# The squares of layer 0's embeddings, summed by ScalarE instead of VectorE, in a two-layer graph network kernel

## The reference

```
layer 0:
  t1    = x @ W1
  msg   = (t1[src] + (x[src] * x[dst]) @ W2) / (sqrt(deg[src]) * sqrt(deg[dst]))
  embed = where(in_cnt > 0, t1 + segment_sum(msg, dst), 0) + b
  embed = leaky_relu(embed, 0.01)
  embed = embed / max(norm(embed, axis=1), 1e-12)
  x1    = layernorm(x + embed)
layer 1:
  out   = segment_sum((x1 @ W.T + b)[src], dst) / (deg + 1)
  y     = layernorm(x1 + out)
```

## Time and profile before

| | |
|---|---|
| Runs | 3945.45, 3954.75, 3956.32 us |
| Median | 3954.75 us |
| Span of the profiled execution | 3955.7 us |
| Busy share TensorE (matmul) | 76% |
| Busy share VectorE | 47% |
| Busy share ScalarE | 17% |
| Busy share GpSimd | 75% |
| Mean granted TensorE clock | 0.742 of full speed |
| Gathers of L585, layer 0 | 1270, from 372.2 us on |
| Gathers of L585, layer 1 | 1540, from 2004.5 us on |

### The profile page before, as it was taken

The page is one execution under the profiler, slowest core; times in us unless marked ns, Lnnn a source line. Parts: engine busy times, 40 slices in busy tenths (PEclk is TensorE's granted clock), DMA queues, the critical chain, the costliest instruction groups (busy, mean ns, idle before and its releaser), DMA issues.

```text
span 3955.7 us, 56274 instructions
## 1 busy us (share of the span) xinstructions
PE 3009.0 (76%) x10186; PEld 1878.7 (47%) x10186; DVE 1854.3 (47%) x3529; ACT 671.9 (17%) x2118; POOL 2958.4 (75%) x3112
## 2 busy tenths in 40 slices
PE   4551887888877778788877888878788878877787
PEld 4441565655556656566534344434444434433443
DVE  9994455555555555555432323233333233323333
ACT  8991111111111111111100000000000000000000
POOL 7776777777777777777757777777777777777776
PEclk5555788888888888887857666677767777677767
DMA  7878455555555555555434444444444444444443
GB/s 254 269 236 318 134 159 158 155 159 160 156 158 158 160 156 160 157 165 157 135 89 118 121 123 122 122 122 122 121 121 121 123 122 121 121 122 122 122 121 107
DMA packets 306368, 588.12 MB, mean 149 GB/s; under 512 B 65107, under 2 KB 189178, under 8 KB 306170
## 3 DMA queue, kind: packets, MB, share of 16 engines
q0 software_dynamic: 148416, 405.47, 35.1%
q1 hardware_dynamic: 144986, 168.09, 12.7%
q10 hardware_dynamic: 12768, 12.85, 0.9%
HBM read 506.24 MB, written 75.45 MB: 147 GB/s over the span
## 4 chain that ended last, share of the span: by engine, by line
POOL 66%; issue 23%; POOLq 1%; DMA 1%; DVE 0%; DVEq 0%; PE 0%; ACT 0%; SPq 0%; ACTq 0%
POOL ring L585 66%; POOLq L582 0%; DMA ring<-scaled_x,idx 0%; DVEq L808 0%; DMA ring<-x,idx 0%; POOLq L583 0%; PE banks L1264 0%; POOL ring L595 0%; DMA x<-out_t 0%; DVE stats L1039 0%; POOLq L627 0%; DMA result<-out_t 0%; DVE out_t L1051 0%; ACT scal L738 0%; POOLq L96 0%
## 5 line engine op out<-in xcount | busy, mean ns | idle before, releaser
L1264 PE MATMUL banks<-ring,hot_space 128*128 128x257 f32 x6252 | 2399.0, 512 | 728.3 <-DMA ring<-x,idx 363.4
L1264 PEld LDWEIGHTS banks<-ring,hot_space 128*128 128x128 f32 x6252 | 1298.5, 238 | 1744.6 <-DMA ring<-x,idx 966.8
L585 POOL DMA_INDIRECT ring<-x,idx x1540 | 1462.1, 949 | 493.7 <-issue 469.2
L585 POOL DMA_INDIRECT ring<-scaled_x,idx x1270 | 1221.2, 962 | 396.5 <-issue 393.7
L970 DVE SCALAR_TENSOR_TENSOR big<-banks,here_mask,big 128x257 f32 x784 | 343.3, 479 | 1693.6 <-PE banks L1264 1693.6
L926 DVE TENSOR_TENSOR hot_space<-banks,dst_rel 128x1024 f32<-128x1024 f32 x392 | 479.6, 1225 | 181.8 <-issue 180.0
L708 ACT COPY idx<-src_col 128x8 int32 (+1 forms) x392 | 77.2, 197 | 2238.8 <-PE banks L1264 2238.8
L595 POOL DMA_INDIRECT ring<-in_x,src_col x276 | 264.9, 960 | 84.1 <-issue 84.1
L671 ACT ACTIVATE dst_rel<-columns,halves 128x128 bf16<-128x128 f32 x960 | 268.3, 375 | 4.6 <-DVE halves L843 4.6
L1163 PE MATMUL banks<-hot_space 128*128 128x98 bf16 x1088 | 101.2, 282 | 132.2 <-DVE hot_space L815 132.2
L1229 PE MATMUL banks<-w_s,a_t 128*128 128x256 f32 x784 | 195.7, 406 | 0.0
(11 more groups left out here) (121 smaller groups left out, 1169.6 us busy)
## 6 DMA issues: line engine op xcount, KB each, us to landing
src_lo<-x SPq DMA_DIRECT2D x2944, 1.0 KB
kept_rows<-ring SPq DMA_DIRECT2D x94, 384.0 KB, 3.2
ring<-kept_rows SPq DMA_DIRECT2D x47, 768.0 KB, 6.0
ring<-x,idx POOLq DMA_INDIRECT x1540, 2.8
src_lo<-scaled_x SPq DMA_DIRECT2D x1408, 1.0 KB
ring<-scaled_x,idx POOLq DMA_INDIRECT x1270, 2.8
dst_col<-in_src SPq DMA_DIRECT2D x47, 384.0 KB, 6.7
scaled_x<-big ACTq DMA_DIRECT2D x14, 896.0 KB, 17.3
```

The lines of the kernel that those rows point to most:

```text
L585: g.indirect_dma_start(ring[:, u, 0:D], None, table[layer], bass.IndirectOffsetOnAxis(ap=idx[:, u:u + 1], axis=0)).then_inc(rows_in[u], 16)
L1264: last = nc.tensor.matmul(group_sum(k % SUMS), dst_hot[:, k % HOTS, u - k * GT, :], ring[:, u, 0:DW], start=u == tiles[0], stop=u == tiles ...
```

## The change

VectorE no longer squares. It increments a semaphore once the leaky relu is done. In `roots` ScalarE waits for that semaphore, increments its own `act_turn`, runs two activations with the function Square over the pair's embeddings, each with its row sums going to the column of `scal` that the root reads, drains, and takes the root as before. The output of the Squares goes to `out_t`, as that of L1003 did. Nothing else changes.

```diff
             def roots(layer, m):
                 if layer == 0:
-                    act.wait_ge(square_ready, m + 1)
+                    act.wait_ge(embed_ready, m + 1)
+                    act.sem_inc(act_turn, 1)
+                    for s in range(2):
+                        nc.scalar.activation(out_t[s][:, :], e[s][:, :], ACT.Square, accum_out=scal[:, 2 + s:3 + s])
+                    act.drain()
                     nc.scalar.activation(pair[2], pair[1], ACT.Sqrt).then_inc(norm_ready, 1)
...
                         nc.vector.scalar_tensor_tensor(e[s][:, :], e[s][:, :], 0.01, e[s][:, :], ALU.mult, ALU.max)
                     ordered()
-                    for s in range(2):
-                        nc.vector.tensor_tensor_reduce(out=out_t[s][:, :], in0=e[s][:, :], in1=e[s][:, :], scale=1.0,
-                                                       scalar=0.0, op0=ALU.mult, op1=ALU.add,
-                                                       accum_out=scal[:, 2 + s:3 + s])
-                    ordered()
-                    v.sem_inc(square_ready, 1)
+                    v.sem_inc(embed_ready, 1)
```

More of the change, by code:

```diff
@@ L267, in gnn @@
         projected = sem("projected")
-        square_ready = sem("square_ready")
+        embed_ready = sem("embed_ready")
         norm_ready = sem("norm_ready")
```

## The result

The kernel after takes 3964.68 us (median of 11 runs, 3963.89 to 3966.67); the kernel before, beside it on the same chip, 3956.01 (11 runs, 3945.45 to 3957.1). The ratio is 1.0024 [1.0015, 1.0032]: slower by 8.7 us, which is less than the 0.3% bound of the prediction and over the top of its range, 3963. The profiled executions have spans of 3964.6 and 3955.7, 8.9 apart, so the two traces hold the difference.

A forecast was written before the change was run, and what follows sets the result against it. The prediction took GpSimd's gathers and the pause ending layer 0 as the bound. Stalls 0 plus end of layer 0 +0.7 gave 3956.4 on the 3955.7 span, carried to the median as 3955.5 us; range 3945 to 3963.

The forecast's parts named there:

- 0.3% bound of the prediction: Whole kernel: 11.9 us, about what a measurement can tell from no change; slower by more was given 0.05.
- I take 0 for all stalls together, -4.8 to +4.2 as bounds: Layer 0's gathers: stalls removed and stalls gained by the shift cancel, net 0 us, between -4.8 and +4.2.
- a replay of layer 0 alone: Layer 0's stall rule replayed with VectorE lines shifted -0.2 to +0.8: 11.8 to 20.8 us of stalls, 16.6 unshifted.
- -1.76 for L1003: Layer 0's gather path: removing the VectorE squares takes away their 16 gather stalls, -1.76 us.
- L1035 and L982 might give it back: Layer 0: these VectorE lines slide onto gather starts, as likely as not giving back L1003's 1.8 us.
- the standing beat: Rival, slower: L1035 and L982 stall gathers nearly every round, up to 0.32 us each, 3969 us; chance 0.03.
- The rule of the stalls: Gathers starting 0.03 us into certain SBUF-only VectorE instructions, over 0.13 before their end, stall until 0.82 past it.
- The price of the pair: Layer 0, leaky relu to root: 1.31 us on ScalarE in place of 0.96, so each pair 0.35 us later.
- The pause: Between layer 0's and layer 1's gathers: two last pairs unhidden, 2 x 0.35 = +0.7 us, 24.9 instead of 24.15.
- The cover: Layer 0: ScalarE's `idx` copy is done at least 12.9 us before its gather, so 0.35 or 0.8 late costs nothing.
- The table switch: Rival: Square outside the roots' table, two loads of 2.57 us per pair, +5.8 at the end, 3961; chance 0.08.
- The rule of the Trainium skill: Prediction read it as L1003 and L984 stalling no gather, -1.76 becoming 0; it went by the trace rows instead.

The follow-up runs named there:

- e1: Kernel after with 25 more drains on VectorE ahead of layer 1's loop; 3952.13 us, 1.0010 of before.
- e2: Kernel before, squares still on VectorE, with 39 more drains on VectorE ahead of layer 1's loop; 3952.4 us, 1.0008 of before.
- e3: Kernel after with layer 1's residual sum reordered so each instruction has an operand in PSUM; 3951.54 us, 1.0008 of before.
- e7: Kernel after with each pair of Squares and its drain done twice; 3955.39 us, 1.0021 of before.
- e6: Kernel after, unchanged, run again on another chip; 3955.33 us, 1.0023 of before.
- e5: Kernel before, unchanged, run again on another chip; 3946.67 us, 0.9999 of before.
- e8: Kernel after without any squares, the root taken of the pair's mask column instead; 3951.01 us, 1.0012 of before.
- e9: Kernel before, squares on VectorE, with only layer 1's residual sum reordered onto PSUM operands; 3947.25 us, 0.9995 of before.
- e10: Kernel after with layer 1's residual sum reordered onto PSUM operands, run again; 3952.11 us, 1.0010 of before.
- e4: Kernel after with layer 1's reordered sum, and layer 0's leaky relu writing to PSUM for Squares and residual sum; 3946.89 us, 0.9995 of before.
- e11: Same edits as e4 (both layers' residual sums with PSUM operands), run again; 3947.71 us, 0.9999 of before.

## Why the prediction was wrong

**What set the time** was named rightly: the gathers of L585, their length and the pause. All but 0.2 of the 8.9 us are there.

**The step that failed** is "I take 0 for all stalls together, -4.8 to +4.2 as bounds". It was made from a replay of layer 0 alone. Layer 1 stood in no term, since no instruction of it was edited, and it gave +5.2 us, the largest part. The mechanism was in the prediction itself (a gather that starts inside certain VectorE instructions waits for their end); what was missing is that the removal shifts VectorE's code, that a gap in it changes by 0.13 us with the place, and that 0.13 us is enough to put L1017's second instruction under the next gather in round after round. e1 and e2 show the place, e3 the stalls.

**The stalls of layer 0.** -1.76 for L1003 came: the line is gone with its stalls. The forecast that L1035 and L982 might give it back held: they stalled 1.0 and 0.1 us before, and 4.1 and 3.7 after (L1034 and L986). The replay gives about 18 against 16.6 at the shift measured, +1.5; the profiled pair has +1.9, the mean of all +2.2. At the shift of e7 it gave 14 and 17.7 were measured, so it does not hold for a large shift. I had taken 0.

The replay moved lines against gathers that stay as they are. The traces show that there is no one shift: from the end of the leaky relu L1034 starts 0.17 us later than L1035 did, in the median, but L986 starts 0.35 later than L982 (9.56 for 9.21; 9.54 for 9.20 in e6 and e5). On the way gathers hold VectorE too. In the trace after:

```profile
599.54 0.95 POOL L585 DMA_INDIRECT ring<-scaled_x,idx  x1 [0.31 <-issue]
...
599.99 0.93 DVE L1050 TENSOR_SCALAR out_t<-out_t,mv,scal 128x256 f32<-128x256 f32 x2
```

The two instructions of L1050 take 0.73 us undisturbed. L1029, of 0.17 us, took over 0.25 in 8 rounds after and 18 in e6, and in none of before or e5. How much of layer 0's +2.2 comes by this way is not shown, and no run took layer 0's squares off VectorE while keeping its phase.

**The rule of the stalls** was read too simply. Its lower bound of 0.03 us holds for the leaky relu. Over the thirteen traces no gather was stalled that began under 0.07 us into L982, 0.077 into L1017, 0.10 into L1035 or 0.12 into L1051; there it is VectorE's instruction that takes longer instead (up to 0.55 us for 0.48 on L1017). So the line of L1017 cost one gather 0.265 us at most in the trace after, where the standing beat was priced at 0.32. Nor does reading SBUF alone make an instruction stall: none of the 483 gathers that began in a BATCH_NORM_STATS2, which has one input, in SBUF, was stalled, as here in the trace after:

```profile
562.75 0.75 DVE L1038 BATCH_NORM_STATS2 stats<-out_t 128x6 f32<-128x256 f32 x2
562.91 0.95 POOL L585 DMA_INDIRECT ring<-scaled_x,idx  x1 [0.30 <-issue]
```

The lines that stall have two tensor inputs in SBUF, or are the TENSOR_SCALAR of L933, L935 and L1051. And L933 also lengthens gathers that were under way when it began, until 0.12 us past its end: six in layer 0 before, 1.1 us.

**The price of the pair** was mis-sized: 0.17 us later, not 0.35. One Square with its read takes 0.42 of ScalarE's time in sequence, where 0.555 was taken: the read of the sums is 0.19 but overlaps.

**The pause** was forecast at +0.7 from 2 x 0.35. At equal work of TensorE it is 0.7, but from other terms: 2 x 0.17, and 0.36 in front of the second residual sum (the 0.45 "issue" of L1034 in the rows above), which is in every kernel with the squares removed from VectorE, e8 too. The other 0.95 us of the profiled pair stand between the last gather and the last group's sum (2.94 us before, 3.89 after). That stretch is 2.9 to 4.1 in both kinds (4.08 in e9, 3.00 in e10), and longer where the products of the last round but one are slow: 4.67 us for 16 at the lower clock after, 3.62 before. It belongs to the execution: of the two kinds either can have the longer one.

**The cover** of 12.9 us over `idx` held, and e7 used 1.1 of it without a trace in the time. **The table switch** did not occur: Square runs under the roots' table. **The rule of the Trainium skill** (SBUF, State Buffer, section "Who interferes with whom"), that a VectorE instruction with two SBUF inputs holds up a GpSimd instruction that reads SBUF and not one that only writes it, was applied wrongly in the prediction. The gather was taken for one that only writes, but `idx`, which it reads, is an SBUF buffer, and stands among the operands in every row of L585. So the stalls on L1017, L984 and L1003, each with two SBUF inputs, agree with the rule, and so does the absence of stalls where one of the two inputs is in PSUM. The Trainium skill infers there that making descriptors needs the write side only; this case does not bear out the conclusion that such an instruction leaves an indirect DMA alone, for L984 stalled 37 gathers by 5.9 us before. That the reading of `idx` is what is held is not shown by any run; e3 and e4 show only that an input moved to PSUM ends the stalls. It also agrees with the account of the Trainium skill there that ScalarE holds up nobody: of the 59 gathers that began during a Square in the traces of after and e6 none was stalled. **The slower rival**, a standing beat, was nearest to what happened; it was given 3 in 100 because I looked for it in layer 0 and priced it to a bound of 11.9 us.

**What stays open.** Why the gap depends on the place of the code is not shown; the experiments show only that it follows the number of instructions ahead. Layer 0's part (+2.2 us) is measured, but that the later root causes it is argued from the rows and not shown by an experiment: the root 1.0 us later still (e7) and 0.8 us earlier than before (e8) gave nearly the same stalls, 17.7 and 17.8 us. Nor is it shown why layer 0's stalls differ by up to 3 us between executions of one kind of kernel.

## What to carry to other kernels

Where GpSimd issues gathers back to back and sets the time, price an edit on VectorE by its phase against them, in every loop of the program and not only in the one that is edited: here a gather that started inside an instruction with two inputs from SBUF waited for its end, and one beside an instruction with an input from PSUM did not. A large part of a difference of 0.2% from removing or adding instructions can be their place alone (here 5 to 6 of some 8 us); the same number of idle instructions put back ahead of the next loop tells it from the work itself. And a matter of layout can be taken out of the comparison by giving such an instruction an operand in PSUM.

## What the runs showed of the hardware that was not expected

- A gap in VectorE's queue of 0.61 or 0.48 us, the same in each of the 44 rounds that run as a loop, by how many instructions lie ahead (25 fewer or 39 more make it 0.48; 25 put back make it 0.61).
- An instruction with both inputs from SBUF stalls a gather even when it writes to PSUM (11 and 15 stalls in e4 and e11); with one input from PSUM there were none, nor in BATCH_NORM_STATS2 with its one input from SBUF (none of 483 gathers).
- It goes both ways: a gather under way made the TENSOR_SCALAR of L1050 end 1.06 us past the gather's start, 0.60 us long for 0.40, in 21 of 47 rounds after and 18 before.
- ScalarE's sum output is an instruction of its own of 0.19 us; a Square of 128x256 with it takes 0.42 in sequence, and from SBUF the pair with its drain 0.98.
- The first chip and the three others differ by 0.003 us in an undisturbed gather, which is 8 us, as much as the change.
